# Linear attention with gated FFNs on one core: order inside the attention step (queries, keys, turned output, values, then state update and output)

## The reference

```python
def step(S, qkv):                      # one chunk of 128 tokens, every head
    qb, kb, vb = qkv
    attn = jnp.where(causal, einsum('bhid,bhjd->bhij', qb, kb), 0.0)
    o = einsum('bhij,bhjv->bhiv', attn, vb) + einsum('bhid,bhdv->bhiv', qb, S)
    S = S + einsum('bhid,bhiv->bhdv', kb, vb)
    return (S, o)
...
o = rmsnorm(o, out_norm_w);  return o @ Wo
```

## Time and profile before

| | |
|---|---|
| time, median of 3 runs | 1176.73 us (1175.73 to 1177.35) |
| the profiled execution's own time | 1174.59 us |
| its span in the profile | 1172.8 us |
| TensorE busy | 1121.0 us (96%), 7364 multiplies |
| TensorE weight loads busy | 1023.2 us (87%) |
| VectorE busy | 860.0 us (73%) |
| ScalarE busy | 512.2 us (44%) |
| mean granted TensorE clock | 0.994 |
| share of TensorE in the chain that ended last | 82%, VectorE 9% |

### The profile page before, as it was taken

The page is one execution under the profiler, slowest core; times in us unless marked ns, Lnnn a source line. Parts: engine busy times, 40 slices in busy tenths (PEclk is TensorE's granted clock), DMA queues, the critical chain, the costliest instruction groups (busy, mean ns, idle before and its releaser), DMA issues.

```text
span 1172.8 us, 21973 instructions
## 1 busy us (share of the span) xinstructions
PE 1121.0 (96%) x7364; PEld 1023.2 (87%) x7364; DVE 860.0 (73%) x1888; ACT 512.2 (44%) x1414; POOL 52.8 (4%) x73
## 2 busy tenths in 40 slices
PE   5999999999998999999999789999999999999998
PEld 4888898898888888988998779999999999999997
DVE  5687777677775876776747787777787777878777
ACT  5544644544544546446454533333333333333332
POOL 1000000000000000000000010202020202020100
PEclk9999999999998999999999999999999999999999
DMA  7322312313322223222222521101020201101110
GB/s 267 95 77 86 112 55 91 100 55 94 101 87 66 94 81 102 67 85 77 58 85 78 180 89 37 54 24 66 18 72 18 72 18 42 48 18 57 33 55 18
DMA packets 100201, 85.92 MB, mean 73 GB/s; under 512 B 7904, under 2 KB 91744, under 8 KB 100064
## 3 DMA queue, kind: packets, MB, share of 16 engines
q1 hardware_dynamic: 100016, 82.66, 22.5%
q0 software_dynamic: 96, 2.16, 0.5%
HBM read 52.73 MB, written 34.23 MB: 74 GB/s over the span
## 4 chain that ended last, share of the span: by engine, by line
PE 82%; DVE 9%; issue 4%; ACT 3%; DMA 2%; SPq 1%; DVEq 0%
PE ps L217 60%; PE ps L573 5%; PE ps L593 4%; PE ps L599 4%; PE ps L560 3%; PE ps L519 2%; PE ps L676 2%; ACT work L813 2%; DVE work L1121 1%; PE ps L620 1%; DMA k_moved<-work 1%; DVE work L1136 1%; PE ps L688 1%; ACT work L823 1%; DMA work<-in_L_attn_Wv 0%
## 5 line engine op out<-in xcount | busy, mean ns | idle before, releaser
L217 PE MATMUL ps<-r_k,r_gate_up 128*128 128x512 f32 x768 | 188.0, 395 | 4.3 <-DVE work L1254 4.3
L217 PEld LDWEIGHTS ps<-r_k,r_gate_up 128*128 128x128 f32 x768 | 141.3, 188 | 32.3 <-DVE work L1254 4.7
L217 PE MATMUL ps<-hT,r_k 128*128 128x512 f32 x384 | 108.6, 420 | 0.9 <-DVE hT L1035 0.9
L217 PE MATMUL ps<-r_o,onT 128*128 128x256 f32 x768 | 107.1, 289 | 0.0
L217 PEld LDWEIGHTS ps<-r_q,r_v 128*128 128x128 f32 x768 | 100.5, 193 | 5.9 <-issue 2.0
L217 PE MATMUL ps<-r_q,r_v 128*128 128x256 f32 x768 | 104.2, 286 | 0.0
L217 PE MATMUL ps<-r_v,hT 128*128 128x512 f32 x384 | 103.6, 406 | 0.0
L217 PE MATMUL ps<-hT,r_q 128*128 128x512 f32 x384 | 100.1, 396 | 0.0
L922 ACT ACTIVATE r_v<-work 128x512 fp32r<-128x512 f32 x64 | 40.5, 633 | 131.3 <-DVE work L1254 131.3
L793 ACT ACTIVATE work<-ps 128x512 f32<-128x512 f32 x64 | 38.4, 599 | 134.0 <-PE ps L217 134.0
L217 PEld LDWEIGHTS ps<-r_o,onT 128*128 128x128 f32 x768 | 95.8, 190 | 0.0
(11 more groups left out here) (132 smaller groups left out, 2051.5 us busy)
## 6 DMA issues: line engine op xcount, KB each, us to landing
k_moved<-work SPq DMA_DIRECT2D x64, 256.0 KB, 2.3
r_gate<-k_moved SPq DMA_DIRECT2D x256, 64.0 KB, 1.9
work<-kept SPq DMA_DIRECT2D x17, 514.0 KB, 5.1
work<-in_L_attn_hidden_states SPq DMA_DIRECT2D x16, 512.0 KB, 4.3
kept<-work SPq DMA_DIRECT2D x9, 514.0 KB, 3.6
work<-kept_xq SPq DMA_DIRECT2D x9, 512.0 KB, 3.7
kept_xq<-work SPq DMA_DIRECT2D x8, 512.0 KB, 3.0
out<-work SPq DMA_DIRECT2D x7, 512.0 KB, 3.3
```

Of the source, the lines that this page charges most:

```text
L217: done = pe.matmul(out_ap, a, b, start=first and n == 0, stop=last and n == 2, skip_group_check=skip)
```

## The change

In TensorE's list the two projections change places (queries first, with their wait for the values' copy), and the state update with its two waits moves from behind the projections to a place behind the turned output and the values. The turns of head 3 stay between the state update and the output. In ScalarE's list the query copy moves ahead of the key copies, and in head 3 the values' copy ahead of the two turned ones. VectorE's and SyncE's lists stay as they are.

```diff
@@ TensorE, attention
                     if not (final and last):
-                        project(wk, B_K, h_next, s_next, k_done)
                         pe.wait_ge(v_ready, min(CH, STEPS - j) + t0 + j if final else t0 + j + CH)
                         project(wq, B_Q, h_next, s_next, q_done)
+                        project(wk, B_K, h_next, s_next, k_done)
+                    if not first or j:
+                        turn_o(t0 + j)
+                    if ahead or h < CH:
+                        pe.wait_ge(q_ready, t0 + j + 2)
+                        values(*((1, h, s) if h < CH else (0, h - CH, 1 - s)))
                     pe.wait_ge(k_tok_ready, t0 + j + 1)
                     if j:
                         pe.wait_ge(state_ready, b * UPDATES + updates_before(j))
@@
                     done.then_inc(ds_done, 1)
-                    if not first or j:
-                        turn_o(t0 + j)
                     if h == CH - 1 and ahead:
...
                         turn_h(1)
-
-                    if ahead or h < CH:
-                        pe.wait_ge(q_ready, t0 + j + 2)
-                        values(*((1, h, s) if h < CH else (0, h - CH, 1 - s)))
@@ ScalarE, attention
                     if not (final and last):
+                        copy_q(t0 + j + 2, (j + 1) % 2)
                         copy_k(t0 + j + 2)
                         act.wait_ge(k_moved_out, 16 * (t0 + j + 1))
                         permute_k()
-                        copy_q(t0 + j + 2, (j + 1) % 2)
@@
+                    if ahead or h < CH:
+                        copy_v(t0 + j + CH + 1, *((1, h) if h < CH else (0, h - CH)))
                     if h == CH - 1 and ahead:
                         turned_hi(0, 1 - s, (n0 + s) * KD + KD + 1)
                         turned_hi(1, 1 - s, (n0 + s) * KD + KD + 2)
-                    if ahead or h < CH:
-                        copy_v(t0 + j + CH + 1, *((1, h) if h < CH else (0, h - CH)))
```

## The result

The changed kernel takes 1187.42 us (median of 4 runs, 1185.88 to 1188.30) against 1176.23 us of the kernel before (4 runs): a ratio of 1.0093, 95% interval 1.0076 to 1.0111. It is 11 us slower. The profiled execution took 1186.8 us with a span of 1185.1, 12.3 more than the span before.

What follows compares the result with a forecast made beforehand. TensorE was taken as the bound, step after step. 20.3 + 5.5 + 2.8 + 1.0 - 17.9 = +11.7 us on 1174.59 made 1186.3, as median 1188.4; forecast 1187.5, 8-in-10 range 1174 to 1203.

Steps and rivals of the forecast that it cites:

- part 1: State update on TensorE: its 18 waits for `turn_k` go, gain 17.9 us, bounds 14.3 and 18.5.
- part 2: Out projection waits for `o_lo`: 27 first-half steps at 0.75 (20.3 us), 26 second-half steps at 0.21 (5.5 us).
- part 3: VectorE's extra work behind `o_lo` holds the next `turn_o` in heads 1 and 3: together 2.8 us, bounds 0 and 8.
- part 4: Other edits: hidden in the loop; in the tail the last update waits about 1.0 us more, bounds 0 and 1.4.
- The first: Rival: the out projection isn't held, so only gain and tail are left, 1160 us; chance 0.09.
- The second: Rival: no change, holds of 0.65 and 0.05 and no tail cost, about 1177 us; chance 0.12.
- The third: Rival: late VectorE turns removed waits into waits of `turn_o` or the update, 1206 us, or 1197; chance 0.14.
- The fourth: Rival: many small holds on TensorE lower the granted clock, 1234 us; chance 0.03.

Runs made afterwards that it cites:

- the experiments on the low part: Changed kernel with the low part of the turned output ahead of VectorE's wait for the state update in every step: 1161.89 us, ratio 0.9873.
- the fourth sum: Changed kernel with the fourth state sum of first halves moved behind the low part of the turned output on VectorE: 1176.75 us, ratio 1.0010.
- The residual's move: Changed kernel with head 1's residual sum moved ahead of VectorE's wait for the state update: 1180.83 us, ratio 1.0033.
- its control: Kernel before the change with head 1's residual sum moved ahead of VectorE's wait for the state update: 1174.24 us, ratio 0.9992.
- both moves: Changed kernel with residual and low part of the turned output ahead of VectorE's wait for the state update: 1158.49 us, ratio 0.9856.
- keys first: Changed kernel with keys projected and copied ahead of queries again, on TensorE and ScalarE: 1210.82 us, ratio 1.0291.
- split values and both moves: Changed kernel with residual and low part ahead of VectorE's update wait, and the update between the two halves of the values: 1158.59 us, ratio 0.9854.
- the old order in its last steps: Changed kernel with keys first and update before turned output in the last four steps only: 1184.08 us, ratio 1.0069.
- the split values and the old tail: Changed kernel with both moves, values split around the update in six heads of first halves, old order in the last four steps: 1151.99 us, ratio 0.9799.
- swap alone: Kernel before the change with only queries projected and copied ahead of keys, update directly behind the projections: 1179.23 us, ratio 1.0032.

## Why the prediction came out as it did

The direction and the two main mechanisms were right. That the time is that of the forecast to 0.1 us, 1187.4 against 1187.5, is luck: several terms were mis-sized or missing, and they cancel. Measured by step lengths, against the span's 12.3:

| term | predicted | measured |
|---|---|---|
| removed waits (part 1) | -17.9 | -20.8, and the first step -0.7 |
| hold in first halves (part 2) | 27 x 0.75 = 20.3 | 27 x 0.65 = 17.6 |
| hold in second halves (part 2) | 26 x 0.21 = 5.5 | 26 x 0.11 = 2.9 |
| head 1 (part 3) | 7 x 0.20 = 1.4 | 7 x 1.13 = 7.9 |
| turned output behind head 3 (part 3) | 3 x 0.45 = 1.4 | 3 x 0.47 = 1.4 |
| the rest of the four steps at the loop's jumps | 0 | about -0.7 |
| start, ahead of the first scores | 0 | 0.4 |
| tail (part 4) | 1.0 | 4.3 |
| sum | 11.7 | 12.3 |

The removed waits are what the steps of the kernel before took beyond 9.37 us (10.24 in head 3, with its turns), apart from the first step, the last three and the four at the loop's two jumps. Those four differ by several us from kernel to kernel, so that term is what remains after the holds and the residual are taken off. The prediction's range from 1181 to 1194 for the forecast isn't explained there: its bounds, added up, give 1177 to 1206.

**Part 1 was right** in mechanism: the waits for `turn_k` are gone but for three, one in the first step and two in the last three. The term was low, since a wait costs more than its idle time plus 0.10. Head 0 of a second half, kernel before, whose scores start at 266.65:

```profile
271.86 0.93 PE L573 MATMUL ps<-work 128*128 128x128 f32 x6 [1.39 <-DVE work L1121]
```

The step is 11.01 - 9.37 = 1.64 us longer than an undisturbed one, 0.25 more than the idle time. The update starts 5.21 behind the scores in place of 3.66, which is 1.55 late: 0.16 more than the bracket shows, and then 0.09 for the restart. Step lengths would have told that beforehand.

**Part 2 was right** in mechanism and in the distances (S + 2.42 and S + 2.96 predicted; 288.30 - 285.90 = 2.40 and 2.95 measured), and the experiments on the low part and on the fourth sum show it. The term that failed is the restart: I carried the 0.10 from the held update, where the multiplies are short, to the out projection, and it isn't paid there. That is 53 x 0.10 = 5.3 us too much. (The lower bound of this part, meant to be without the restart, counts 0.05 for a second half; 0.21 less 0.10 is 0.11, and with that it is 20.4, against 20.5 measured.)

**Part 3 named the wrong wait in head 1.** I took the extra work of head 1 to matter only for the next turned output. Its first instruction, the residual, is read by somebody much sooner: the out projection of the same step waits for it. The section on the kernel before names the residual in head 1 and the earlier trace rows its 1.22 us; what I skipped, there and in the prediction, was the second wait ahead of the out projection, the one for `x2_summed`. The rule for an added cover (name who waits for every instruction that is pushed back) was applied to the low part and not to what stands behind it. The residual's move and its control show the term. Head 3's term was right.

**Part 4, the tail.** The last update came 5.62 us behind the last scores in place of 4.20, 1.4 for the predicted 1.0. What I missed is what followed. TensorE was idle for 1.42 and again for 2.49 us, and from the update on it ran at half the clock. The changed kernel's last steps:

```profile
659.33 1.05 PE L560 MATMUL ps<-work 128*128 128x128 f32 x8
...
661.81 0.66 PE L519 MATMUL ps<-ident,work 128*128 128x128 f32 x4 [1.42 <-DVE work L1183]
...
664.95 1.65 PE L578 MATMUL ps<-work 128*128 128x128 f32 x6 [2.49 <-DVE work L1120]
...
669.66 1.90 PE L217 MATMUL ps<-r_o,onT 128*128 128x256 f32 x12
```

and busy time by stretch, columns as in the earlier trace rows, of the changed kernel and then of the kernel before behind its own last wait:

```profile
664.00:669.60 5.60, 4.65 (x22) 4.65 (x23) 2.18 (x5) 0.00 (x0) 0.00 (x0) 0.50 0.64 201
```

```profile
655.50:660.00 4.50, 4.48 (x39) 4.49 (x40) 1.68 (x5) 1.85 (x10) 0.00 (x0) 1.00 0.73 198
```

From the update to the out projection it took 4.71 us in place of 2.91, 1.8 more, although the turned output no longer lies between the two. With the same order and a granted clock of 1.00 the kernel with both moves took 639.71 - 637.23 = 2.48, so the lower clock cost 2.2 us here. With the update's 1.4 that makes 3.2 of the tail's 4.3; the remaining 1.1 lies behind the start of the last out projection and wasn't taken apart.

**The rivals.** The first (no hold) falls: the hold is there. The second (both ends low) falls with it. The third (VectorE turns removed waits into others) is right in head 4 of first halves only, where a wait of the turned output (L519 for L1183 in the waits above) cost 0.47 and so took back the 0.45 won there. The fourth (the clock falls from many small holds) falls for the loop: with some fifty holds of 0.1 to 1.3 us the granted clock is 0.99 from 31 to 663 us, and 1.00 from 225 to 340, between two jumps. The Trainium skill ("TensorE: Matmul & The Clock Gate", section "A second HAM failure mode: psum-queue depth-cycling") tells of a kernel whose frequent short idle times between groups made the clock swing; these holds didn't. In the tail the clock did fall, and also in kernels that wait there only once (table at the end).

What failed in an experiment's expectation is named there: the range of the low part's move, the restart of 0.1 in the run with keys first, the price of `turn_k`'s return in the run with split values and both moves, and the clock in the run with the old order in its last steps.

## What to carry to other kernels

Moving a producer next to its consumer on the busiest engine takes the cover from the whole chain on the other engine, and from everything queued there behind the chain: list each of these instructions and look for who waits for it, even where the present trace shows no wait. If the chain holds work that doesn't need the moved producer (here the low part and the residual), move it ahead of the wait in the same edit; that turned 0.9% slower into 1.4% faster, and the split values and the old tail made it 2.0%. Price a wait by the distance of block starts, not by the idle time in brackets.

## What I had not expected of the hardware

- The idle time shown in front of a held block of multiplies was 0.16 to 0.44 us less than its delay, taken from the starts of the blocks: 1.39 for 1.55 ahead of the state update (head 0 of a second half), 0.97 for 1.22 ahead of the out projection (head 1, changed kernel), 0.19 for 0.63 there in a first half, 0.25 for 0.50 ahead of the values (keys first).
- What is lost beyond the delay depends on what follows. The steps grew by 1.64, 1.24, 0.65 and 0.52, so 0.09 more than the delay ahead of the update and 0.02 ahead of the other two. Inside the output of a first half a held state multiply lost 0.10 as well. The two places that pay are blocks of 128x128 multiplies; whether that is the reason wasn't tested.
- The lower clock follows neither from the length of the last idle time nor from their number. Behind the last scores, one execution each:

| kernel | TensorE idle ahead of the last update | granted clock, 5.5 us from the update on | update to out projection |
|---|---|---|---|
| before | 3.15 | 1.00 | 2.91 |
| before, residual early | 2.52 | 1.00 | 2.91 |
| swap alone | 4.31 | 0.71 | 4.45 |
| old order in the last four steps | 2.78 | 0.69 | 4.55 |
| both moves | 0.95, 1.80 | 1.00 | 2.48 |
| low part alone | 0.95, 1.48 | 0.69 | 4.10 |
| fourth sum late | 1.42, 2.52 | 0.74 | 3.85 |
| changed | 1.42, 2.49 | 0.53 | 4.71 |

In the first four the turned output lies between update and out projection, in the others between the two idle times. The changed kernel and the one with the fourth sum late have the same order and nearly the same idle times, and differ by 0.9 us; so the price of the clock in this tail isn't fixed. What decides it stays open.
